# A causal mask added by VectorE on the way to its maximum, in place of matmuls

## The chip, the core and the metric

The kernel runs on one core of a Trainium2 chip. The metric is the device time of one execution in microseconds, the median of several runs.

## What is computed

16 batch entries of 128 tokens and 256 features go through four stages; x is kept in float32 and each stage adds to it.

```python
x = x + xattn0(layernorm(x), ctx, ctx)          # stage A: 32 heads of 8, 8 KV heads
x = x + moe(layernorm(x), ...)                  # stage B: top 2 of 8 experts, and a shared one
x = x + xattn1(layernorm(x), ctx, Wq, Wkv, Wo)  # stage C: 16 heads of 16, causal
x = x + ffn(layernorm(x), w1, w2)               # stage D: quantised, 256 -> 1024 -> 256
```

Stage C, which the change touches:

```python
qh, kh, vh = heads(q @ Wq.T), heads(k), heads(v)
scores = einsum('bhqd,bhkd->bhqk', qh, kh) * inv_sqrt_d
scores = where(tril(ones), scores, finfo.min)
out = einsum('bhqk,bhkd->bhqd', softmax(scores), vh) @ Wout.T
```

## The kernel before

A batch entry is a tile: 128 tokens on the 128 partitions. Each stage is cut into parts (A0 to A6, B0 to B6, C0 to C10, D0 to D4), and a part into what each engine does of it. PROGRAMS (lines 84 to 211) holds, for each engine, a hand-written list of parts with their tiles, as "C4.0/3": half 0 of part C4 of tile 3. An engine walks its list in order, and no engine looks ahead in it. So several tiles are under way at once, in different stages, and what joins the engines are semaphores. `s.wait` waits for the result of a part.

TensorE writes into two rings of PSUM slots: four small ones (one bank each) and two big ones (two banks, 1024 float32 columns). PARTS (lines 67 to 80) says for each part which ring it uses and which semaphore count frees its slot. `fill` (line 405) takes the next slot of the ring in the order of TensorE's list and waits until the part that had it before is read. The users of the big ring are A2, A4, B2, B3, B4, C4, C6 and D2.

The softmax needs each row's maximum before the exponential. Stage C finds it so:

1. C4 on TensorE (line 712), two halves of eight heads: the scores q k with the queries on the partitions, in float32 parts of bfloat16 (96 rows). Ahead of them two matmuls of 512 columns put the mask (0 or -3e38, bfloat16) into the slot through an identity, and the heads accumulate upon it.
2. C4 on VectorE (line 1220, `neg_max` at 1212): one reduce over 128x1024, straight from PSUM, gives the negated maxima of eight heads and frees the slot.
3. C4 on POOL (line 1102): the 16 maxima are split into two bfloat16 parts.
4. C5 on TensorE (line 729) transposes them, C5 on ScalarE (line 874) copies them out, C5 on the DMA queue (line 540) writes them as two more rows behind QC.
5. C6 on TensorE (line 734) makes the scores again, now with the keys on the partitions and the maximum subtracted by the two extra rows. ScalarE (line 934) takes the exponential, POOL (line 1126) sets what the mask forbids to 0, and C7 to C10 multiply by the values, normalise, project and add.

Stage A does the same in its parts A2 to A4 without a mask; its reduces (line 1214) share the helper with stage C's. Stage D's quantiser takes maxima of 256 and 1024 columns (line 1204), its D2 writes z (line 1299) and D4 scales the output (line 1308). Stage B's routing is ten small VectorE steps (lines 1244 to 1262), with two products behind them (1234, 1266), and B3 and B4 multiply by halves of 512 columns (1234, 1273).

zbuf is 2 x 1024 float32 columns. It first holds weights of stage D (f1, f2) until their signs and scales are taken, then its first half is z.

## Time and profile before

| | us |
|---|---|
| median of 3 runs | 603.13 |
| lowest, highest | 598.46, 604.03 |
| the profiled execution's own time | 601.62 |
| its span, first to last instruction | 599.6 |

The span is that of the profiled execution; 2.0 us lie around it. Durations are from this one execution. The profile gives an engine's busy time (an instruction's latency counts in it, so matmuls one behind the other overlap), the idle time in front of a group and what ended it, and the chain that ended last.

### The profile page before, as it was taken

How to read it: one execution, taken by the hardware profiler on the slowest of the kernel's cores; microseconds unless marked ns; L12 is line 12 of the kernel's file. 1: busy time of each engine (PE TensorE's matmuls, PEld its weight loads, DVE VectorE, ACT ScalarE, POOL GpSimd, SP SyncE). 2: the span in 40 equal slices, each digit the busy share in tenths (PEclk: the TensorE clock that was granted, in tenths of full speed). 3: DMA queues.
4: the chain of work that ended last, by engine and by line, in shares of the span. 5: the costliest groups of instructions: out<-in, count | busy, mean ns of one | idle time of the engine just before them, and what ended most of it. 6: DMA issues, size and time to landing. Idle time of an engine off the chain costs nothing.

```text
span 599.6 us, 10827 instructions
## 1 busy us (share of the span) xinstructions
PE 523.7 (87%) x3860; PEld 326.9 (55%) x3874; DVE 353.5 (59%) x768; ACT 397.7 (66%) x755; POOL 279.5 (47%) x536
## 2 busy tenths in 40 slices
PE   3477889899988988999799999999999999997764
PEld 1243465565655557575447565665646565674532
DVE  3643746565767674666556667576677366636342
ACT  5164344548874968575976876769677678747655
POOL 3996724365444353554435444562523443363220
PEclk9677979999999999999899999999999999999886
DMA  6788610413132220313040410432130302023000
GB/s 174 178 262 188 152 52 17 110 33 98 41 78 63 70 67 28 100 40 96 25 116 14 118 26 25 108 80 59 29 84 20 84 16 67 11 61 103 25 0 17
DMA packets 66444, 43.97 MB, mean 73 GB/s; under 512 B 36616, under 2 KB 61064, under 8 KB 66392
## 3 DMA queue, kind: packets, MB, share of 16 engines
q1 hardware_dynamic: 60064, 37.56, 24.9%
q10 hardware_dynamic: 6328, 5.73, 3.4%
q8 instruction: 31, 0.51, 0.4%
q14 instruction: 21, 0.17, 0.1%
HBM read 30.49 MB, written 12.39 MB: 71 GB/s over the span
## 4 chain that ended last, share of the span: by engine, by line
PE 54%; ACT 21%; DVE 12%; POOL 4%; issue 4%; DMA 3%; SPq 1%; POOLq 0%; ACTq 0%
PE big L651 16%; PE small L684 8%; PE small L630 4%; ACT PA L880 3%; ACT PC L880 3%; PE small L767 3%; DVE neg_maxA L1214 2%; PE big L603 2%; ACT L880 2%; PE small L588 2%; PE small L797 2%; PE big L780 2%; PE big L618 2%; PE small L749 2%; ACT g L965 2%
## 5 line engine op out<-in xcount | busy, mean ns | idle before, releaser
L1214 DVE TENSOR_REDUCE neg_maxA<-big 128x8 f32<-128x1024 f32 x64 | 77.0, 1215 | 25.6 <-PE big L603 25.1
L904 ACT ACTIVATE tB<-big,route_half 128x128 f32<-128x128 f32 x128 | 36.5, 367 | 58.9 <-PE big L651 58.9
L880 ACT ACTIVATE PA<-big 128x1024 f32<-128x1024 f32 x64 | 64.2, 1030 | 16.1 <-PE big L618 16.0
L1121 POOL TENSOR_TENSOR vB<-vB,route_c 128x512 f32<-128x512 f32 x32 | 33.3, 1039 | 82.0 <-DVE vB L1273 81.9
L684 PE MATMUL small<-w2T,hTB 128*128 128x256 f32 x288 | 66.9, 387 | 2.6 <-ACT hTB L917 2.6
L651 PE MATMUL big<-w1T,xTB 128*128 128x512 f32 x128 | 61.3, 601 | 5.2 <-DVE vB L1266 3.4
L684 PEld LDWEIGHTS small<-w2T,hTB 128*128 128x128 f32 x288 | 54.4, 193 | 11.8 <-issue 3.0
L651 PE MATMUL big<-w3T,xTB 128*128 128x512 f32 x128 | 60.2, 592 | 0.0
L1234 DVE SCALAR_TENSOR_TENSOR tB<-tB,big 128x512 f32<-128x512 f32 (+1 forms) x48 | 26.3, 548 | 41.9 <-ACT tB L904 41.9
L1129 POOL TENSOR_SCALAR_AFFINE_SELECT PC<-PC 128x1024 f32<-128x1024 f32 x32 | 35.0, 1097 | 32.4 <-ACT PC L880 32.4
L1214 DVE TENSOR_REDUCE neg_maxC<-big 128x8 f32<-128x1024 f32 x32 | 38.4, 1216 | 13.9 <-PE big L725 13.7
L651 PEld LDWEIGHTS big<-w3T,xTB 128*128 128x128 f32 x128 | 24.3, 190 | 30.6 <-issue 30.6
L651 PEld LDWEIGHTS big<-w1T,xTB 128*128 128x128 f32 x128 | 22.3, 190 | 28.0 <-issue 19.7
L603 PE MATMUL big<-KA,QA 48*128 48x128 bf16 x512 | 25.9, 229 | 12.8 <-DVE neg_maxA L1214 4.0
L880 ACT ACTIVATE PC<-big 128x1024 f32<-128x1024 f32 x32 | 32.7, 1029 | 5.0 <-PE big L740 4.8
L630 PE MATMUL small<-PA,VA 128*32 128x512 f32 x256 | 35.2, 644 | 0.7 <-ACT PA L880 0.7
L618 PE MATMUL big<-QA,KA 50*128 50x512 bf16 x128 | 25.3, 412 | 9.7 <-DVE neg_maxC L1214 3.1
L603 PEld LDWEIGHTS big<-KA,QA 48*128 48x128 bf16 x512 | 15.7, 98 | 28.9 <-DVE neg_maxA L1214 8.5
L1299 DVE SCALAR_TENSOR_TENSOR z<-big,qscale,f_scale 128x1024 f32<-128x1024 f32 x16 | 20.5, 1280 | 10.4 <-PE big L780 10.3
L888 ACT ACTIVATE OA<-small 128x512 f32<-128x512 f32 x32 | 19.3, 602 | 10.1 <-PE small L630 9.8
L917 ACT ACTIVATE hTB<-small 128x512 f32<-128x512 f32 (+1 forms) x48 | 23.4, 505 | 3.1 <-PE small L675 2.7
L675 PE MATMUL small<-ident,vB 128*128 128x128 f32 x144 | 23.3, 281 | 1.4 <-DVE vB L1266 0.8
(195 smaller groups left out, 1202.8 us busy)
## 6 DMA issues: line engine op xcount, KB each, us to landing
parts_qA<-QP SPq DMA_DIRECT2D x16, 192.0 KB, 2.4
QA<-parts_qA SPq DMA_DIRECT2D x32, 96.0 KB
parts_kC<-KPC SPq DMA_DIRECT2D x16, 192.0 KB, 2.2
KC<-parts_kC SPq DMA_DIRECT2D x16, 192.0 KB, 2.9
parts_qC<-QPC SPq DMA_DIRECT2D x16, 192.0 KB, 2.1
QC<-parts_qC SPq DMA_DIRECT2D x16, 192.0 KB, 2.9
x<-in_x SPq DMA_DIRECT2D x16, 128.0 KB, 2.4
QA<-parts_qA SPq DMA_DIRECT2D x32, 64.0 KB
```

The costliest lines, as they stand in the source:

```text
L603: last = mm(ps[:, c * BANK + g * P:c * BANK + (g + 1) * P], QA[u][rows, G0 * j + g, :], KA[rows, t // KCHUNK, j, t % KCHUNK * P:(t % KCHUN ...
L618: last = mm(ps[:, c * BANK:(c + 1) * BANK], KA[rows, t // KCHUNK, j, t % KCHUNK * P:(t % KCHUNK + 1) * P], QA[u][rows, G0 * j:G0 * (j + 1) ...
L630: last = mm(ps[SLOT * j:SLOT * (j + 1), :], VA[u][:, kv, :], PA[:, kv * G0:(kv + 1) * G0, :], start=True, stop=True)
L651: last = mm(ps[:, o:o + n], xTB[u][:, c, :], w[c], start=(c == 0), stop=(c == DC - 1))
L684: last = mm(ps[:, 0:D], hTB[:, e, :], w_2[:, e, :], start=(e == 0), stop=(e == NE - 1))
L880: return op(dst[:, 8 * j:8 * (j + 1), :], ps[:].rearrange("p (h t) -> p h t", t=P), ACT.Exp, scale=scale).then_inc(S[name], 1)
L904: ins = op(tB[:, (e0 + i) * HID:(e0 + i + 1) * HID], ps[:, i * HID:(i + 1) * HID], ACT.Tanh, scale=rt["half"][:, e0 + i:e0 + i + 1])
L917: op(hTB[:, e0:e0 + n, :], ps[:, 0:n * P].rearrange("p (e t) -> p e t", t=P), ACT.Copy)\
L1121: g.tensor_tensor(hB[:, sl].rearrange("p (e h) -> p e h", e=4), vB[:, sl].rearrange("p (e h) -> p e h", e=4), rt["c"][:, e0:e0 + 4].unsque ...
L1129: g.affine_select(out=p, in_=p, compare_op=ALU.is_ge, fill=0.0, base=0, pattern=[[0, 8], [1, P]], channel_multiplier=-1).then_inc(S["PC_ca ...
L1214: v.tensor_reduce(dst[:, 8 * j:8 * (j + 1)], ps[:].rearrange("p (h t) -> p h t", t=P), FREE, ALU.max, negate=True).then_inc(S[name], 1)
L1234: return v.scalar_tensor_tensor(out=uB[:, lo:lo + n], in0=tB[:, lo:lo + n], scalar=1.0, in1=ps[:, 0:n], op0=ALU.add, op1=ALU.mult)
```

## The change

C4 on TensorE issues no mask matmuls; each head's matmul starts and stops its own accumulation. C4 on VectorE adds the mask from SBUF to the slot and writes the sum to the second half of zbuf, named sC. It then takes the maximum from there. The slot is free after the add: PARTS names the semaphore sC for C4. The lists of parts stay. VectorE waits for its own reduce before it overwrites sC, and for its own add before it reads it; in tile 0 it also waits for the mask and for zbuf. TensorE's wait for the constants goes from C4 to C6.

```diff
-    ... "C4.0": (1, "nmC", 2, 1),
-    "C4.1": (1, "nmC", 2, 2), ...
+    ... "C4.0": (1, "sC", 2, 1),
+    "C4.1": (1, "sC", 2, 2), ...
-        z = zbuf[:, 0, :]
+        z, sC = zbuf[:, 0, :], zbuf[:, 1, :]
...
             def C4(s, t, u, j):
                 ps, full = s.fill()
-                if t == 0 and j == 0:
-                    pe.wait_ge(S["consts"], 3)
                 if j == 0:
                     s.landed("KC_in", t, 3)
                     s.landed("QC_in", t, 3)
-                for b in range(2):
-                    mm(ps[:, b * BANK:(b + 1) * BANK], identb[:], mask[:].unsqueeze(1).broadcast_to([P, 4, P]),
-                       start=True, stop=False)
-                for b in range(2):
-                    for i in range(4):
-                        h = 8 * j + 4 * b + i
-                        last = mm(ps[:, b * BANK + i * P:b * BANK + (i + 1) * P], QC[u][0:K1, h, :], KC[u][0:K1, h, :],
-                                  start=False, stop=(i == 3))
+                for i in range(8):
+                    h = 8 * j + i
+                    last = mm(ps[:, i * P:(i + 1) * P], QC[u][0:K1, h, :], KC[u][0:K1, h, :], start=True, stop=True)
                 last.then_inc(full, 1)
...
             def C6(s, t, u, j):
                 ps, full = s.fill()
+                if t == 0 and j == 0:
+                    pe.wait_ge(S["consts"], 3)
...
             def C4(s, t, u, j):
-                neg_max(s, j, nmC[u], "nmC")
+                ps = s.read()
+                if t == 0 and j == 0:
+                    dve.wait_ge(S["consts"], 3)
+                    dve.wait_ge(S["f2_sign"], 2)
+                if t or j:
+                    dve.wait_ge(S["nmC"], 2 * t + j)
+                heads = sC.rearrange("p (h t) -> p h t", t=P)
+                v.tensor_tensor(heads, ps[:].rearrange("p (h t) -> p h t", t=P), mask[:].unsqueeze(1).broadcast_to([P, 8, P]),
+                                ALU.add).then_inc(S["sC"], 1)
+                dve.wait_ge(S["sC"], 2 * t + j + 1)
+                v.tensor_reduce(nmC[u][:, 8 * j:8 * (j + 1)], heads, FREE, ALU.max, negate=True).then_inc(S["nmC"], 1)
```

## Rows read from the trace of the kernel before

**Rows 1.** The page's first part: busy time, share of the span, instructions.

```profile
PE 523.7 (87%) x3860; PEld 326.9 (55%) x3874; DVE 353.5 (59%) x768; ACT 397.7 (66%) x755; POOL 279.5 (47%) x536
```

**Rows 2.** Stretches: us; engines' busy us; TensorE's granted clock, DMA share, GB/s.

```profile
130.00:545.00 415.00, 387.83 (x2998) 250.01 (x3009) 260.74 (x587) 302.97 (x587) 191.04 (x375) 1.00 0.24 60
200.00:300.00 100.00, 91.93 (x714) 58.10 (x716) 64.19 (x139) 73.02 (x140) 45.62 (x95) 0.98 0.25 63
545.00:575.00 30.00, 23.16 (x221) 14.28 (x220) 14.54 (x26) 20.04 (x26) 10.28 (x19) 0.94 0.19 50
575.00:600.00 25.00, 13.04 (x62) 6.99 (x63) 9.12 (x20) 13.77 (x18) 2.45 (x5) 0.73 0.03 10
```

**Rows 3.** The page's chain that ended last, by engine.

```profile
PE 54%; ACT 21%; DVE 12%; POOL 4%; issue 4%; DMA 3%; SPq 1%; POOLq 0%; ACTq 0%
```

**Rows 4.** Groups by line, TensorE: busy us, mean ns | idle before.

```profile
L720 PE MATMUL big<-mask,identb 128*128 128x512 bf16 x64 | 19.2, 381 | 1.2 <-ACT PA L880 0.5 <-DVE z L1299 0.5 <-ACT PC L880 0.2
...
L732 PE MATMUL small<-identb,neg_max2C 128*32 128x128 bf16 x16 | 3.6, 226 | 0.1
```

**Rows 5.** Timeline, tile 0's C4: start us, duration, instruction.

```profile
109.30 0.59 PE L720 MATMUL big<-mask,identb 128*128 128x512 bf16 x2
109.73 0.61 PE L725 MATMUL big<-KC,QC 96*128 96x128 bf16 x8
...
110.38 2.35 DVE L1214 TENSOR_REDUCE neg_maxC<-big 128x8 f32<-128x1024 f32 x2 [2.52 <-PE big L725]
...
112.98 0.63 PE L651 MATMUL big<-sw1T_gateT,xTB 128*128 128x136 f32 x4
```

**Rows 6.** Groups by line, VectorE.

```profile
L1214 DVE TENSOR_REDUCE neg_maxC<-big 128x8 f32<-128x1024 f32 x32 | 38.4, 1216 | 13.9 <-PE big L725 13.7
...
L1273 DVE TENSOR_TENSOR vB<-tB,big 128x512 f32<-128x512 f32 x32 | 22.0, 687 | 1.1
L1299 DVE SCALAR_TENSOR_TENSOR z<-big,qscale,f_scale 128x1024 f32<-128x1024 f32 x16 | 20.5, 1280 | 10.4 <-PE big L780 10.3
L1204 DVE TENSOR_REDUCE qscale<-g 128x1 f32<-128x1024 f32 x16 | 19.4, 1210 | 6.3 <-ACT g L965 6.3
...
L1290 DVE TENSOR_TENSOR oC<-small,rlC 128x256 f32<-128x256 f32 x16 | 6.8, 424 | 0.6
```

**Rows 7.** Line 1179: duration ns min/median/max, first and last start.

```profile
L1179 DVE SCALAR_TENSOR_TENSOR f2q<-g,f2q x1: 1601/1601/1601, 46.5 to 46.5; 128x1024 bf16<-128x1024 f32 x1
```

**Rows 8.** Timeline, C4, C5, C6 of tiles 14 and 15.

```profile
549.30 1.21 DVE L1214 TENSOR_REDUCE neg_maxC<-big 128x8 f32<-128x1024 f32 x1
...
550.42 1.21 DVE L1204 TENSOR_REDUCE qscale<-g 128x1 f32<-128x1024 f32 x1
...
551.21 0.22 PE L732 MATMUL small<-identb,neg_max2C 128*32 128x128 bf16 x1
...
551.66 0.15 DVE L1205 TENSOR_SCALAR qscale<-qscale 128x1 f32<-128x1 f32 x1
...
556.76 0.62 PE L740 MATMUL big<-QC,KC 98*128 98x128 bf16 x8 [0.76 <-DMA QC<-neg_maxT_C]
...
558.30 1.23 DVE L1214 TENSOR_REDUCE neg_maxC<-big 128x8 f32<-128x1024 f32 x1 [1.05 <-PE big L725]
...
561.99 0.22 PE L732 MATMUL small<-identb,neg_max2C 128*32 128x128 bf16 x1
...
563.14 1.86 PE L797 MATMUL small<-f2q,gT 128*128 128x256 bf16 x8 [0.93 <-ACT gT L976]
```

**Rows 9.** Timeline, C4 and C5 of tile 2.

```profile
169.05 2.35 DVE L1214 TENSOR_REDUCE neg_maxC<-big 128x8 f32<-128x1024 f32 x2 [2.69 <-PE big L725]
...
172.42 0.23 PE L732 MATMUL small<-identb,neg_max2C 128*32 128x128 bf16 x1
```

**Rows 10.** Timeline, TensorE behind C5 of tile 6.

```profile
293.52 0.23 PE L732 MATMUL small<-identb,neg_max2C 128*32 128x128 bf16 x1
...
295.24 0.40 PE L603 MATMUL big<-KA,QA 48*128 48x128 bf16 x8 [1.48 <-ACT PA L880]
```

More of the change, by code:

```diff
@@ L377, in build @@
             "xTC", "qTC", "kTC", "VC", "qpC", "kpC", "qpC_out0", "qpC_out1", "kpC_out0", "kpC_out1", "QC_in0", "QC_in1", "KC_in0", "KC_in1",
-            "nmC", "nm2C", "mTC", "mrowsC", "PC", "PC_causal", "OC", "rlC", "oC", "oTC", "x3_done",
[1 row of a table added]
             "qs1", "yq", "yT", "z", "g", "g2", "gq", "gT", "y2", "x4_done")}
```

5 rows, old and new, of tables (PARTS, S) are left out of this document.

## The prediction, made before the change was run

> **What bounds the kernel now.** I read the page's busy line first [rows 1]: TensorE is busy 87% of the span, VectorE 59%, ScalarE 66%. The table of stretches then says where [rows 2]: between 130 and 545 us TensorE is busy 387.8 of 415 us, 93%, at a granted clock of 1.00, ScalarE 73% and VectorE 63%. From 545 us on TensorE is busy 77%, then 52%. The chain of work that ended last is 54% TensorE, 21% ScalarE, 12% VectorE [rows 3]. So TensorE, walking a fixed list of parts, sets the pace in the middle; behind 545 us it is the latency of one tile's chain, and VectorE lies in it.
>
> That seems to invite the change, for it takes work from TensorE and gives it to an engine with 246 us of idle time. But TensorE's list is in order, and it waits for VectorE's result four parts or so after it asked for it. So the question is how much room there is between the end of C4's maxima and the part C5 that transposes them.
>
> **What goes.** Each of the 32 C4 parts loses two mask matmuls of 512 columns. The group shows 381 ns for one, 19.2 us busy in all [rows 4], but that counts the latency of each part's first matmul; what they hold is the distance between starts: 109.30 for the masks, 109.73 for the heads behind them, 0.43 us [rows 5]. That is 32 x 0.43 = 13.8 us of TensorE. They stand behind all of C4's waits, so no wait hides them. The eight head matmuls stay as they are.
>
> **What comes.** Each C4 gains one VectorE add, 128x1024 in float32, PSUM and the bfloat16 mask in, SBUF out. No such row exists. The nearest are adds and products with one operand in PSUM: 687 ns for 512 columns, 424 for 256 [rows 6], so 1.03 ns a column and 1.21 us for 1024. The one-operand pass over 1024 from PSUM takes 1.22, the three-operand one 1.28. The low end is 0.69 us, the 512-column row, if repeating the short mask over the heads somehow halved the price; the high end is 1.60 us, the slowest pass over 1024 with bfloat16 in it [rows 7]. I take 1.21, the row of the same kind. The reduce now reads SBUF: the same length from SBUF takes 1.21 against 1.22 [rows 6], no change.
>
> The two self-waits: behind a reduce the next instruction without a wait starts 1.12 us after it (549.30, 550.42), the one that waits for it 1.24 (550.42, 551.66) [rows 8]. So add to reduce is 1.24, and a pair that stands together goes from 2.35 to 3 x 1.24 + 1.21 = 4.93 us: 2.6 more. VectorE in all gains 32 x 1.27 = 41 us, 353 to 394, 65% of the span; no bound by itself. The page "VectorE: DVE Perf Modes" of the Trainium skill, section "The DRAIN you can't avoid", says that a semaphore between two operations costs nothing extra. By it the pair would be 4 x 1.12 + 0.09 = 4.57, a third of a microsecond less a tile. The two starts above speak against it, so the sum keeps 1.24.
>
> The waits on the mask's constants and on the staging buffer fall on tile 0 at 110 us, when both are long done; the last pass that needs the signs is over by 49 us [rows 7]. The mask wait moved to C6 costs nothing for the same reason. POOL's select behind the exponentials stays, and no DMA is added.
>
> **What it does to the order.** The PSUM slot now comes free after the add (1.21) and no more after the reduce (1.22). For the first C4 of a pair that is no loss and, where VectorE waited for TensorE, 0.43 early. For the second it comes one reduce later. The result of the pair is late by D: 2.6 where the pair stands together and VectorE was busy anyway; 2.6 - 0.43 = 2.15 where it waited for the matmuls, as in tile 2 [rows 9]; 1.24 or 0.8 where only the second reduce still matters, because the two stand apart.
>
> The shortest way from a reduce's end to C5 is 0.70 us (550.51 to 551.21 [rows 8]): two POOL instructions and their semaphores. Slack is C5's start less the reduce's end less 0.70. Tile 2 is the type [rows 9]: reduces end at 171.40, C5 at 172.42, slack 0.32, D = 2.15, so C5 starts 1.8 later than before, and TensorE, which would have been there 0.86 early, stands for 2.7. Behind it in VectorE's list come C10, D0, D4 and two reduces of stage A; they are 2.15 late as well, which is no worse than C5.
>
> By the same reading of all 16 tiles (C4's and C5's rows, of which [rows 5, 8, 9, 10] show the first, the last two, a typical one and an absorbed one), TensorE is later than before by: tile 0 0.7 (C5 has 4 us of slack, but B2 wants the slot of the second C4 at 112.98 and gets it at 110.38 - 0.43 + 2 x 1.24 + 1.21 = 113.64 [rows 5]); 1 0.7; 2 1.8; 3 0.8; 4 0.4; 5 0.1; 6 0.65; 7 0.6; 8 0.2; 9 0; 10 1.3; 11 0.5; 12 -0.5 (slack 4.1, the gain stays); 13 1.3. Tile 6 shows why it isn't D less slack everywhere, which would be 2.3 there: TensorE stood for 1.48 us before 295.24, until ScalarE had read a PSUM slot [rows 10], so 1.7 of the 2.3 vanish. The sum is 8.6 us. The 13.8 us of TensorE are already in it: each C5 comes 0.86 early, and that time is spent waiting.
>
> Tiles 14 and 15 are on the chain. For tile 14 the last chain runs through VectorE: z, maximum, quantiser, maximum, quantiser, then ScalarE [rows 8]. Two adds and their waits go in, 2 x 1.24 = 2.5 us, nothing hides them; the other way out, C5 to the row DMA to C6 at 556.76, was waited for too and is as late. Tile 15: add from 557.87, reduce until 560.32, D4's pass of 0.48, add from 560.8, reduce until 563.3, C5 at 564.0 in place of 561.99; but D4 behind it in TensorE's list waited until 563.14 for ScalarE anyway, so 0.9 [rows 8]. Together 3.4 us.
>
> Of the 8.6 us some comes back. Between 130 and 545 us TensorE is idle 27 us [rows 2], many of the pieces waits for ScalarE, which doesn't slow down. A TensorE that is 1 us late finds such a wait 1 us shorter, as at tile 6. I let half return: 4.3 + 3.4 = 7.7 us. The span goes to 607.3, and with the 2.0 us around it (601.62 against 599.6) to 609.3. The profiled execution lay 1.5 us under the median of the runs shown (603.13); from that median the forecast is 610.8. I give 610, +1.1%.
>
> **Rivals.** (a) TensorE's gain wins, faster. It needs the waits at C5 to be short: an add well under 1.2 us, or the pieces of slack growing because all other parts of VectorE get ahead. Then 13.8 us times TensorE's busy share in the middle, 0.93, less the 3.4 us of the tail, -9.5: about 592 to 595. For it speaks that TensorE is the busiest engine and VectorE has a third of its time free; against it the slack under 1 us in ten of 16 tiles. It decides where the second result is late by less than about 0.8 us. Chance 0.13.
> (b) All cancels in the middle: ScalarE's waits take up the whole 8.6, and only the tail is left: +3, 605 to 606. Chance 0.27. ScalarE's 73% in the middle speaks for it [rows 2].
> (c) VectorE's lateness spreads, slower by much more. Each second C4 holds up what is behind it in the list: stage A's 64 reduces, which free the two large PSUM slots, and the ten small routing steps before B2's products, which are on the chain today. If tiles that stand together pay the full 2.6 and those apart 1.2 with nothing coming back, 7 x 2.15 + 9 x 0.8 less what is hidden gives +15 to +20: 617 to 622. A little of it could be TensorE's clock: the whole middle has 1.00 at 93% busy, the stretch from 200 to 300 us 0.98 at 92% [rows 2], and 2% of a slower clock on a stretch of 100 us is at most 2 us. Against (c): VectorE is idle over 3 us in every 10. Chance 0.15.
> (d) That the change doesn't take the matmuls away, or that they cost nothing today, I exclude: they have rows of their own, and nothing waits in front of them for more than 1.2 us in all [rows 4].
>
> **The numbers.** Forecast 0.45, with its own range of 605 to 616. A measurement of this kernel tells about 1% from no change, that is 597.1 and 609.2. Faster is (a), 0.13. Within 1%: (b) and a third of the forecast's share, 0.25 + 0.13 = 0.38. Slower the rest, 0.49. The range for 8 in 10 takes in (b) and most of (c), and leaves out (a): 600 to 619. The ends of the add's price (0.69, 1.60) move the sum by 32 x 0.4 x about a third, some 4 to 6 us, which fits inside.
>
> **What would show it.** Right: C5's transpose (line 732, moved) has a wait for POOL's copy of the maxima of 1 to 2.5 us in most tiles, some 15 to 20 us in all, where before it had 0.1 [rows 4]; TensorE's busy time falls by 14 to 19 us and its idle time grows by more; the add takes 1.2 us, VectorE is busy some 392 us; the stretch from C4 of tile 14 to the end is 3 us longer. Wrong: no wait at C5, TensorE's busy share unchanged in the middle and the span shorter (then a), or C5's waits there, but ScalarE's waits of TensorE gone and the span the same (then b).

## The result, and the profile after

The changed kernel takes 620.97 us (median of 4 runs, 619.31 to 622.37), the kernel before 602.0 on the same chip (598.46 to 604.03): a ratio of 1.0322, 95% interval 1.0276 to 1.0368. So 19 us slower, where the forecast was 610 us (7.7 us more of span) with a range of 600 to 619. A ratio is taken over the single runs of a kernel and of the kernel before on the same chip, and can lie up to 0.3% beside that of the medians. A few executions fall into a slower state of the chip and stay out of every ratio, here two of x8's ten, its profiled one among them. The profiled execution took 620.25 us, its span is 618.5, 18.9 more than before. First the page's busy line and its chain by engine:

```profile
PE 518.8 (84%) x3796; PEld 323.3 (52%) x3810; DVE 390.7 (63%) x800; ACT 398.9 (64%) x755; POOL 279.4 (45%) x536
...
PE 47%; DVE 24%; ACT 16%; issue 5%; DMA 4%; POOL 3%; SPq 1%; POOLq 0%; DVEq 0%
```

VectorE's busy time is up by 37.2 us (the adds are 39.0), and its share of the chain has doubled against [rows 3]. TensorE's busy time fell by 4.9 us only [rows 1]. Span less busy time is its idle time: 75.9 us before, 99.7 now. These 23.8 us less 4.9 are the 18.9 of the span, so the place to look is what ends TensorE's waits. Groups by line (line, operation, out<-in, count | busy us, mean ns | idle time before them, and what ended it):

```profile
L725 PE MATMUL small<-identb,neg_max2C 128*32 128x128 bf16 x16 | 3.7, 229 | 11.4 <-POOL neg_max2C L1089 11.4
...
L618 PE MATMUL big<-QA,KA 50*128 50x512 bf16 x128 | 25.7, 419 | 15.3 <-DVE z L1224 8.0 <-DMA QA<-neg_maxT_A 3.3 <-ACT PA L875 2.6
...
L588 PE MATMUL small<-ident,oC 128*128 128x128 f32 x32 | 6.6, 287 | 3.2 <-DVE oC L1296 3.1
...
L719 PE MATMUL big<-KC,QC 96*128 96x128 bf16 x256 | 19.4, 220 | 3.5 <-ACT PA L875 1.3 <-ACT PC L875 1.0 <-DVE z L1305 0.9
```

The first is C5, where the forecast looked: 11.4 us of waiting in place of 0.1 [rows 4]. The second is a part of stage A (A4, its second scores matmul) that fills a large PSUM slot. In the kernel before the same group reads:

```profile
L618 PE MATMUL big<-QA,KA 50*128 50x512 bf16 x128 | 25.3, 412 | 9.7 <-DVE neg_maxC L1214 3.1 <-ACT PA L880 2.6 <-DMA QA<-neg_maxT_A 2.3
```

So it waits 5.6 us more, and what grew is the wait until C4 has read its slot, from 3.1 to 8.0 us. The third stands behind VectorE's normalisation of stage C (0.4 before). The fourth is C4 itself (1.2 before, on the mask's row [rows 4]). So half of the new idle time, 11.3 of 23.8 us, stands at C5, the other half elsewhere.

VectorE's two new groups, and the timeline of tile 2, which the prediction took as its type [rows 9]:

```profile
L1224 DVE TENSOR_TENSOR z<-big,mask 128x1024 f32<-128x1024 f32 x32 | 39.0, 1218 | 7.8 <-PE big L719 6.9
...
L1227 DVE TENSOR_REDUCE neg_maxC<-z 128x8 f32<-128x1024 f32 x32 | 39.0, 1220 | 1.1
```

```profile
170.47 0.62 PE L719 MATMUL big<-KC,QC 96*128 96x128 bf16 x8 [0.52 <-ACT PA L875]
171.13 1.22 DVE L1224 TENSOR_TENSOR z<-big,mask 128x1024 f32<-128x1024 f32 x1 [2.25 <-PE big L719]
171.38 0.62 PE L719 MATMUL big<-KC,QC 96*128 96x128 bf16 x8 [0.29 <-ACT PA L875]
172.23 0.41 PE L588 MATMUL small<-ident,xnC 128*128 128x128 f32 x2 [0.23 <-ACT xnC L856]
172.39 1.22 DVE L1227 TENSOR_REDUCE neg_maxC<-z 128x8 f32<-128x1024 f32 x1
...
173.71 1.23 DVE L1224 TENSOR_TENSOR z<-big,mask 128x1024 f32<-128x1024 f32 x1
...
174.97 1.22 DVE L1227 TENSOR_REDUCE neg_maxC<-z 128x8 f32<-128x1024 f32 x1
...
176.91 0.21 PE L725 MATMUL small<-identb,neg_max2C 128*32 128x128 bf16 x1 [1.91 <-POOL neg_max2C L1089]
```

The starts of add, reduce, add, reduce are 1.26, 1.32 and 1.26 us apart, and the pair takes 5.06 us (171.13 to 176.19) for 2.35 before. TensorE, ahead by the four mask matmuls that are gone (0.86 us), spends 0.29 and 0.23 us of that on two new waits for ScalarE, and then waits 1.91 us at C5.

The middle, as in [rows 2]:

```profile
130.00:545.00 415.00, 370.60 (x2846) 237.66 (x2857) 287.31 (x600) 295.09 (x567) 181.79 (x360) 0.99 0.23 57
```

In the middle TensorE is busy 89% in place of 93%. The end, tiles 14 and 15, from the timeline:

```profile
565.90 1.23 DVE L1224 TENSOR_TENSOR z<-big,mask 128x1024 f32<-128x1024 f32 x1
...
567.16 1.22 DVE L1227 TENSOR_REDUCE neg_maxC<-z 128x8 f32<-128x1024 f32 x1
...
569.08 0.27 PE L725 MATMUL small<-identb,neg_max2C 128*32 128x128 bf16 x1 [1.58 <-POOL neg_max2C L1089]
...
577.92 1.21 DVE L1224 TENSOR_TENSOR z<-big,mask 128x1024 f32<-128x1024 f32 x1
...
579.17 1.22 DVE L1227 TENSOR_REDUCE neg_maxC<-z 128x8 f32<-128x1024 f32 x1
...
581.09 0.26 PE L725 MATMUL small<-identb,neg_max2C 128*32 128x128 bf16 x1 [0.80 <-POOL neg_max2C L1089]
```

C5 of tile 15 is 19.1 us later than in [rows 8]. The table below gives that for every second tile or so: the start of C5's matmul in this kernel's timeline less its start before. It has four of the experiments too, which come later.

```
tile                                0    2    4    6    8   10   12   13   15
changed kernel                    1.7  4.5  6.9  9.4  9.6 11.3 13.7 15.4 19.1
x1  no mask, no add               0.7  2.3  3.1  2.4  2.1  1.2  0.8  0.8  0.7
x14 no mask in tiles 7-13         2.5  2.5  2.5  2.4  2.8  1.9  1.6  1.5  1.5
x9  spare reduce behind C4's      1.6  2.3  5.3  7.5  9.7 10.1 12.4 12.5 14.7
x12 spare reduce ahead of C4's    5.1  7.7  9.1 12.9 16.2 18.5 21.5 22.6 25.9
```

Read the steps along a row, not its first number (each is one execution): x14 runs the same instructions as before up to tile 6 and is 2.5 us late from the start, which is the difference between two executions.

One step of the changed kernel is not VectorE's. From tile 3 to tile 4 it loses 1.9 us, and 1.6 of them lie in one group of 18 matmuls of stage B (line 684), which took 4.12 us before. First the kernel before, then the changed one, with a stretch inside the group. Third from its end stands the granted clock, the share of TensorE's full speed of 2.4 GHz that it was given:

```profile
225.96 4.12 PE L684 MATMUL small<-w2T,hTB 128*128 128x256 f32 x18 [0.55 <-ACT hTB L917]
```

```profile
231.00 5.75 PE L684 MATMUL small<-w2T,hTB 128*128 128x256 f32 x18 [0.93 <-ACT hTB L912]
...
232.00:236.00 4.00, 4.00 (x15) 3.35 (x14) 0.32 (x3) 3.96 (x6) 1.10 (x1) 0.71 0.00 0
```

The clock fell there. In windows of 4 us between 100 and 545 us the trace of before has one such fall (296 to 300 us), the changed kernel's has four (108, 228, 300 and 448 us, each some 8 us long). TensorE's busy time in each such window, times what is missing of the full clock, is 1.6 us in all before and 6.0 now.

### The profile page after: what moved, and what is told of

The parts are those of the page before. It is cut to its first block, busy times and chain, and to the rows that moved or that the text cites. A ratio compares the mean times of both kernels' runs of the same rounds, so it can differ in the third digit from the quotient of the medians.

```text
span 618.5 us, 10763 instructions
## 1 busy us (share of the span) xinstructions
PE 518.8 (84%) x3796; PEld 323.3 (52%) x3810; DVE 390.7 (63%) x800; ACT 398.9 (64%) x755; POOL 279.4 (45%) x536
## 4 chain that ended last, share of the span: by engine, by line
PE 47%; DVE 24%; ACT 16%; issue 5%; DMA 4%; POOL 3%; SPq 1%; POOLq 0%; DVEq 0%
PE big L651 15%; PE small L684 8%; DVE z L1224 5%; DVE neg_maxC L1227 5%; PE small L630 4%; DVE neg_maxA L1209 3%; ACT PA L875 2%; PE small L762 2%; ACT PC L875 2%; PE big L603 2%; PE big L775 2%; ACT g L960 2%; PE big L618 1%; PE small L705 1%; PE small L675 1%
## 5 line engine op out<-in xcount | busy, mean ns | idle before, releaser
L1224 DVE TENSOR_TENSOR z<-big,mask 128x1024 f32<-128x1024 f32 x32 | 39.0, 1218 | 7.8 <-PE big L719 6.9
L1227 DVE TENSOR_REDUCE neg_maxC<-z 128x8 f32<-128x1024 f32 x32 | 39.0, 1220 | 1.1
L883 ACT ACTIVATE OA<-small 128x512 f32<-128x512 f32 x32 | 19.1, 601 | 9.7 <-PE small L630 9.7
```

The lines of the kernel that those rows point to most:

```text
L1224: v.tensor_tensor(heads, ps[:].rearrange("p (h t) -> p h t", t=P), mask[:].unsqueeze(1).broadcast_to([P, 8, P]), ALU.add).then_inc(S["sC"], 1)
L1227: v.tensor_reduce(nmC[u][:, 8 * j:8 * (j + 1)], heads, FREE, ALU.max, negate=True).then_inc(S["nmC"], 1)
```

## The experiments

Three things were open. Which part of the 19 us is VectorE's load, which is C4's result being late, and which its PSUM slots? What is the taking of 13.8 us from TensorE worth? And what has TensorE's clock to do with it, since its mean is 0.938 to 0.946 in the runs of the changed kernel and 0.955 in the profile of before?

### The two halves of the change, each alone

**x1: the masks' matmuls gone, no add.** The kernel before, its C4 without the mask matmuls. The maxima are then over all keys; the select behind the exponentials still masks.

```diff
-                for b in range(2):
-                    mm(ps[:, b * BANK:(b + 1) * BANK], identb[:], mask[:]...)
...
+                for i in range(8):
+                    h = 8 * j + i
+                    last = mm(ps[:, i * P:(i + 1) * P], QC[u][0:K1, h, :], KC[u][0:K1, h, :], start=True, stop=True)
```

> The kernel before without its mask matmuls, and with no add: the maximum is taken over all keys, also those that the causal mask forbids (the select behind the exponentials still sets those to 0). It measures what TensorE's part of the change is worth alone. If TensorE's 13.8 us count in full where it sets the pace: 589 to 591 us against 602. If TensorE only comes earlier to waits for others, so that the saving is worth little: 598 to 602. The changed kernel's 621 is then this time plus what VectorE's add costs.

Measured: 603.57 us (10 runs) beside 601.38, ratio 1.001 (0.9975 to 1.0045). 13.8 us less of TensorE's work changed nothing clear of the noise (1.5 us less to 2.7 more), which is near the second of the two expectations. Groups of this run:

```profile
L618 PE MATMUL big<-QA,KA 50*128 50x512 bf16 x128 | 24.9, 402 | 12.4 <-DVE neg_maxC L1209 5.1 <-DMA QA<-neg_maxT_A 3.1 <-ACT PA L875 2.6
...
L721 PE MATMUL big<-KC,QC 96*128 96x128 bf16 x256 | 19.4, 219 | 3.7 <-ACT PA L875 1.3 <-ACT PC L875 1.1 <-DVE z L1294 0.9
...
L727 PE MATMUL small<-identb,neg_max2C 128*32 128x128 bf16 x16 | 3.6, 227 | 0.5 <-POOL neg_max2C L1089 0.5
```

C5 hardly waits, so its slack was there. But the slots' waits grew from 9.7 to 12.4 us and C4's own from 1.2 to 3.7: TensorE gets to a slot sooner and finds it not yet read.

**x2: both.** The changed kernel with the mask matmuls put back as before (the lines that x1 takes out); the mask's constant is -1e38 in place of -3e38, since it is now added twice.

> The changed kernel with the mask matmuls put back in front of the heads (the mask is added twice, at -1e38 each, so no value overflows): VectorE's part of the change alone. If the two parts simply add up, this is 621 plus what the matmuls' removal is worth: 632 to 634 if that is 12 us, 623 if it is 2. If the removal made the waits at C5 longer (TensorE comes 0.86 us a tile too early and stands there), its worth in this company is far less than alone: 621 to 625 while the kernel without any mask is at 590.

Measured: 629.39 us (4 runs), ratio 1.0441 (1.039 to 1.0492), so VectorE's half of the change costs 26 to 28 us by itself. From x2 to the changed kernel (1.0441 to 1.0322) the same matmuls are worth some 7 us, give or take 4, and alone nothing. The two halves don't add, and x2 lies between the two cases that were expected.

**x4 and x5: one C4 of the two.** The add for the first (x4) or the second C4 of each tile only (x5), the other one as before.

```diff
             def C4(s, t, u, j):
+                if j != 0:          # x5: j != 1
+                    return neg_max(s, j, nmC[u], "nmC")
                 ps = s.read()
```

> The change for the first half of C4 alone: its mask is added by VectorE, the second half keeps its mask matmuls, its plain reduce and its slot freed by the reduce. The theory of the joints (what counts is how late C5's input and the second slot are) expects little where the two halves stand apart, for the first add is then over long before: 603 to 608. The theory of the load (each microsecond on VectorE costs its share wherever it lies) expects half of the whole change: 610 to 612.

> The change for the second half of C4 alone. Its add lies between the matmuls and C5 in every tile. The theory of the joints expects most of the loss here: 612 to 617. The theory of the load expects the same as for the first half, 610 to 612.

Measured: x4 609.71 us, ratio 1.012 (1.0096 to 1.0145); x5 610.69 us, ratio 1.0129 (1.0088 to 1.0171), 4 runs each. By the medians that is 8.3 and 9.3 us, together 17.6 of the 19; by the ratios 7.2 and 7.8, together 15.0 of 19.4. An add in front of the first maximum costs about as much as one in front of the second. Had the lateness of the tile's result been all, the first would have to be the cheaper one, since where the two C4 stand apart only the second reduce matters to C5: 603 to 608 us were expected for it by that, against 612 to 617. The intervals (1.5 us either way for x4, 2.5 for x5) leave room for a small difference only.

### VectorE's load against its late result

**x9 and x12: a spare reduce.** The kernel before, with one more VectorE reduce for each C4, over 8x127 columns of an idle staging buffer, that nobody reads. In x9 it stands behind C4's reduce, so C4's first slot and maxima are in time (the second only where the two stand apart) and what is behind comes 1.2 us later; in x12 ahead of it, behind the wait for the matmuls, so that every slot and maximum of C4 is later by 1.2 us more. The masks stay on TensorE.

```diff
             def C4(s, t, u, j):
                 neg_max(s, j, nmC[u], "nmC")
+                ...
+                v.tensor_reduce(zbuf[:, 1, HF - 8:], zbuf[:, 1, 0:HF - 8].rearrange("p (h t) -> p h t", t=P - 1), FREE, ALU.max,
+                                negate=True).then_inc(S["sC"], 1)      # x12: ahead of neg_max, behind s.read()
```

> The kernel before, mask matmuls and all, with a spare VectorE reduce over 8x127 columns of the idle staging buffer behind each C4 reduce (its result is used by nobody): 32 x 1.2 us more on VectorE, but C4's own slot and maxima come as before, except where the second half stands directly behind the first one's spare. If it is VectorE's load that costs, whatever the microseconds are spent on: 625 to 630, as VectorE's part of the change alone (629). If it is the lateness of C4's own results: 605 to 612.

> The same spare reduce ahead of each C4 reduce, behind the wait for the matmuls: the same load, and C4's slot and maxima 1.2 us a half later. Load theory: the same time as with the spare behind. Theory of late results: 635 to 642, since here the slot is late as well (that cost 11 us in the changed kernel).

Measured: x9 614.01 us, ratio 1.0195 (1.0145 to 1.0245); x12 624.95 us, ratio 1.0374 (1.0319 to 1.043); 4 runs each, beside 601.96. So 38.4 us of load behind the results cost 12.0 us, and in front of them another 10.9. Neither theory had this: 614 lies between what late results (605 to 612) and load (625 to 630) gave for x9, 625 between what they gave for x12. Nor is x9 load alone, since in the eight tiles where the two C4 stand together its second slot and maxima are 1.2 us late. First x9's groups, then x12's:

```profile
L1226 DVE TENSOR_REDUCE z<-z 128x8 f32<-128x1016 f32 x32 | 38.4, 1201 | 0.0
...
L618 PE MATMUL big<-QA,KA 50*128 50x512 bf16 x128 | 26.0, 424 | 12.5 <-DVE neg_maxC L1214 5.4 <-DMA QA<-neg_maxT_A 3.4 <-ACT PA L880 2.4
...
L732 PE MATMUL small<-identb,neg_max2C 128*32 128x128 bf16 x16 | 3.7, 232 | 1.2 <-POOL neg_max2C L1094 1.1
```

```profile
L618 PE MATMUL big<-QA,KA 50*128 50x512 bf16 x128 | 25.3, 412 | 21.5 <-DVE neg_maxC L1214 13.0 <-DMA QA<-neg_maxT_A 4.5 <-ACT PA L880 2.4
...
L732 PE MATMUL small<-identb,neg_max2C 128*32 128x128 bf16 x16 | 3.7, 230 | 7.4 <-POOL neg_max2C L1094 7.3
```

In x9 C5 waits 1.2 us in all, and the kernel is still 12 us slower; the slot group waits 2.8 us more than before, the rest is spread over other groups. In x12 the slot group alone waits 9 us more than in x9, C5 6.2 more.

**x3: the slot.** The changed kernel, but the PSUM slot counts as free only when the reduce is done, not the add.

```diff
-... "C4.0": (1, "sC", 2, 1), "C4.1": (1, "sC", 2, 2), ...
+... "C4.0": (1, "nmC", 2, 1), "C4.1": (1, "nmC", 2, 2), ...
```

> The changed kernel with C4's PSUM slot freed by the reduce and not by the add: the same work and order, the slot 1.24 us later. It prices the slots. If the big ring is a joint that counts: 630 to 640, for 32 slots are each 1.24 us later. If VectorE's load alone counts: 621 to 624.

Measured: 631.73 us (4 runs), ratio 1.05 (1.0443 to 1.0557), against 1.0322: slots that come some 1.26 us later cost 11 us more, as the theory of the slots had it (630 to 640).

```profile
L618 PE MATMUL big<-QA,KA 50*128 50x512 bf16 x128 | 24.8, 401 | 22.1 <-DVE neg_maxC L1227 16.7 <-ACT PA L875 2.4 <-DVE neg_maxA L1209 1.5
...
L725 PE MATMUL small<-identb,neg_max2C 128*32 128x128 bf16 x16 | 3.9, 244 | 7.6 <-POOL neg_max2C L1089 7.5
```

The slots' wait for C4 doubles from 8.0 to 16.7 us; C5's shrinks from 11.4 to 7.6, for TensorE is already late when it gets there.

**x6: C5 later in TensorE's list.** The changed kernel with C5 one to four parts later in 14 tiles (for tile 2: behind A2.3, A5.0 and A5.1 in place of ahead of them).

```diff
-        C4.0/2 C4.1/2 C1/3 C10/1 B1/4 D4/0 A2.2/6 C5/2 A2.3/6 A5.0/5 A5.1/5 A2.0/7 ...
+        C4.0/2 C4.1/2 C1/3 C10/1 B1/4 D4/0 A2.2/6 A2.3/6 A5.0/5 A5.1/5 C5/2 A2.0/7 ...
```

> The changed kernel with C5 moved one to six parts later in TensorE's list in 14 of the 16 tiles (not 1 and 14), so that up to about 2 us of other matmuls come ahead of it. It takes away the waits of C5 for the maxima (11.4 us in the changed kernel). If C5's waits are what the change costs: 609 to 612 against 621. If the cost is VectorE's load, met at whatever joint comes next: 618 to 622, with C5's waits gone and others longer.

Measured: 629.64 us (4 runs), ratio 1.0473 (1.0409 to 1.0536), 9 us worse than the change it was to mend, and outside both expectations (609 to 612, 618 to 622). In this kernel line 726 is C5:

```profile
L726 PE MATMUL small<-identb,neg_max2C 128*32 128x128 bf16 x16 | 3.8, 238 | 3.6 <-POOL neg_max2C L1090 3.6
...
L652 PE MATMUL big<-w1T,xTB 128*128 128x512 f32 x128 | 63.5, 620 | 7.4 <-DVE vB L1273 5.5 <-DVE neg_maxA L1210 1.9
...
L652 PE MATMUL big<-sw1T_gateT,xTB 128*128 128x136 f32 x64 | 12.4, 321 | 3.6 <-ACT PA L876 1.6 <-DVE neg_maxA L1210 1.0 <-ACT xTB L888 1.0
```

C5's wait went from 11.4 to 3.6 us, and other parts, wait longer (line 652: 7.4 and 3.6 for 5.1 and 1.3). Moved in this way, the wait at C5 was where the lateness showed, not where it could be taken off; other orders were not tried.

**x11: both adds first.** The changed kernel with the masked scores in bfloat16, so that two fit the staging buffer; in the eight tiles where the two C4 stand together the order is add, add, reduce, reduce, and no instruction waits for the one right ahead of it.

```diff
+                if together and j == 0:
+                    return
+                for i in ((0, 1) if together else (j,)):
+                    dve.wait_ge(S["sC"], 2 * t + i + 1)
+                    v.tensor_reduce(nmC[u][:, 8 * i:8 * (i + 1)], heads[i], FREE, ALU.max, negate=True).then_inc(S["nmC"], 1)
```

> The changed kernel with sC in bfloat16, two of them in the same bytes, so that in the seven tiles whose halves stand together (0, 1, 2, 5, 6, 7, 10, 13: eight with 5) VectorE does both adds first and then both reduces: the second slot comes free 1.24 us earlier, the first maximum 1.24 later, the last as before. In the other tiles nothing moves. Slots as a joint that counts (11 us for 32 slots 1.24 us later): 3 us less, 617 to 618. Load: 621.

Measured: 619.55 us (4 runs), ratio 1.029 (1.0242 to 1.0338); the interval overlaps the change's. Tile 2 in its timeline:

```profile
169.24 2.36 DVE L1226 TENSOR_TENSOR z<-big,mask 128x1024 bf16<-128x1024 f32 x2 [2.26 <-PE big L719]
171.51 2.33 DVE L1232 TENSOR_REDUCE neg_maxC<-z 128x8 f32<-128x1024 bf16 x2
```

The four take 4.60 us (169.24 to 173.84) in place of 5.06. Eight tiles of 0.46 us are 3.7 us of latency less, of which 1.4 show, and these are within the error: x11 can't tell the 617 to 618 of the slots from the 621 of the load.

### Shortening in place of lengthening

**x8 and x10.** x8 is the kernel before with C4's reduce over 64 of each head's 128 keys, which takes 16 us off VectorE (337.7 us busy in x10's profile, 353.5 before; a piece of the computation is left out); x10 is x8 and x1 together.

```diff
-                neg_max(s, j, nmC[u], "nmC")
+                ps = s.read()
+                v.tensor_reduce(nmC[u][:, 8 * j:8 * (j + 1)], ps[:].rearrange("p (h t) -> p h t", t=P)[:, :, 0:P // 2], FREE, ALU.max,
+                                negate=True).then_inc(S["nmC"], 1)
```

> The kernel before with C4's reduce cut to the first 64 of 128 keys of each head (the maximum leaves out the other keys; nothing else changes): VectorE has 32 x 0.53 = 17 us less to do. VectorE's part of the change cost 28 us for 40 us of work, 0.7 for 1. If that slope holds in both directions, VectorE paces the kernel already: 602 - 12 = 590. If the order of the lists is fitted to today's durations, so that longer hurts and shorter doesn't help, as with the mask matmuls: 599 to 602.

> The kernel before with both cuts at once: no mask matmuls (the maximum takes in forbidden keys) and C4's reduce over 64 of 128 keys. TensorE has 13.8 us less, VectorE 17 us less. Each alone gave nothing. If the two engines' lists hold each other, so that each alone only waits longer for the other: 588 to 595. If something else holds both (ScalarE, whose list is untouched, or the chain of one tile at the end): 599 to 603.

Measured: x8 601.12 us beside 602.78, ratio 0.9974 (0.9935 to 1.0012); x10 602.1 us beside 601.96, ratio 1.0001 (0.9971 to 1.0032), 10 runs each. Neither engine's work, nor both together, gives anything clear of the noise when it shrinks, as the expectation of fitted lists had it.

### The clock

**x7: C5's waits filled.** The changed kernel with 42 dummy matmuls ahead of C5 and C9 in the tiles where they wait, so that TensorE is busy there.

```diff
-    A4.0/1:10 C2.1/0:4 ...
+    C5/1:2 C5/2:7 C5/3:2 C5/6:3 C9/4:4 C5/10:6 C9/8:3 C9/11:2 C5/13:5 C5/14:6 C5/15:2 A4.0/1:10 C2.1/0:4 ...
```

> The changed kernel with 42 idle matmuls (the kernel's own fillers, 512 columns, result unused) put into the waits of C5 and C9 that its trace shows, each a little shorter than the wait. It adds no work that matters and keeps TensorE active. If part of the loss is TensorE's granted clock (0.94 over the runs of the changed kernel, 0.96 over those of before): the clock rises to 0.95 or more and the time falls to 613 to 617. If the clock plays no part: 621, or 1 to 3 us more.

Measured: 622.33 us (4 runs), ratio 1.0362 (1.0299 to 1.0426). The granted clock of the four runs is 0.946 to 0.958, against 0.938 to 0.946, and the time is not better. The clock rose as foretold for the case that it is part of the loss, but the 613 to 617 us of that case did not come; 622 is what was expected if the clock plays no part. The C5 group:

```profile
L725 PE MATMUL small<-identb,neg_max2C 128*32 128x128 bf16 x16 | 3.7, 234 | 3.6 <-POOL neg_max2C L1089 2.9 <-ACT gT L971 0.7
```

**x13 and x14: where the masks go.** With all masks gone (x1) the clock fell to about half (0.50 to 0.53 in windows of 2 us) in three places of the middle, before only in one (296 to 300 us). x13 leaves the masks out in 13 tiles and keeps them in tiles 2, 4 and 6, just ahead of those places; x14 leaves them out in tiles 7 to 13 alone, where x1's clock stood at 1.00. Maxima over all keys in the tiles without masks.

```diff
-                for b in range(2):
-                    mm(...mask...)
+                if t in (2, 4, 6):          # x14: t < 7 or t > 13
+                    ...as before
+                else:
+                    ...as x1
```

> The kernel before with the mask matmuls left out in 13 tiles (26 x 0.43 = 11.2 us of TensorE less) and kept in tiles 2, 4 and 6, just ahead of the three stretches in which TensorE's granted clock fell when all were gone (168 to 176, 228 to 232, 296 to 304 us: together about 6.8 us of TensorE at full clock, against 1.7 before). In those 13 tiles the maxima are over all keys; the select behind the exponentials still masks. If the clock ate the gain, the falls at 168 and 228 are away, the transpose of the maxima is no more 1.6 and 1.4 us late behind tiles 2 and 4, and the time is 3 to 5 us under that with all masks gone: 598 to 600. If waits side by side ate it, moving a fall changes little: the same time as with all gone, 601 to 604, the lateness per tile about as before at +1 to +3.

> The kernel before with the mask matmuls left out in tiles 7 to 13 only (14 x 0.43 = 6.0 us of TensorE less, maxima over all keys there), where the clock stood at 1.00 with all of them gone. The parts ahead of tile 7 run as before, with the one fall at 296. If the clock is what takes the gain elsewhere, most of the 6 us shows by tile 13's transpose of the maxima: 3 to 5 us early, 597 to 599. If waits for ScalarE and VectorE take it, as in the run with all gone (from 2.8 late at tile 7 to 0.8 at tile 13, 2.0 us gained by six tiles), 2 us early or less, and 600 to 602 in all.

Measured: x13 601.39 us, ratio 0.9993 (0.9975 to 1.001); x14 599.73 us, ratio 0.9965 (0.9946 to 0.9984), beside 601.76, 12 runs each. x14 is the only kernel of the study whose interval lies below the one before, by 2.0 us (1.0 to 3.3). First x1's stretches (granted clock third from the end), then x13's, x14's, and the last of the kernel before:

```profile
172.00:176.00 4.00, 4.00 (x37) 2.38 (x40) 2.56 (x5) 1.19 (x3) 1.93 (x5) 0.77 0.10 33
228.00:232.00 4.00, 4.00 (x12) 3.23 (x11) 0.17 (x2) 3.99 (x5) 0.66 (x1) 0.57 0.00 0
...
344.00:520.00 176.00, 166.60 (x1303) 106.67 (x1302) 114.87 (x257) 133.97 (x253) 78.32 (x151) 1.00 0.21 54
```

```profile
172.00:176.00 4.00, 4.00 (x47) 2.60 (x49) 3.93 (x8) 2.19 (x6) 1.59 (x6) 1.00 0.44 99
228.00:232.00 4.00, 4.00 (x26) 3.35 (x26) 0.36 (x2) 3.99 (x5) 0.79 (x1) 1.00 0.00 0
```

```profile
344.00:520.00 176.00, 165.96 (x1292) 106.61 (x1295) 115.47 (x262) 133.90 (x252) 77.67 (x149) 1.00 0.21 54
```

```profile
344.00:520.00 176.00, 167.89 (x1321) 108.32 (x1326) 113.15 (x250) 133.80 (x252) 77.93 (x150) 1.00 0.20 53
```

In x13 the falls at 172 and 228 us are away, and tiles 2 and 4 don't step back by 1.6 and 1.4 us as in x1. But other falls came, at 112 and 336 us, and in all they take as much as x1's: TensorE's busy time times the missing clock, in the windows of 4 us, is 6.1 us in x13, 5.9 in x1, 2.6 in x14. So x13 moved the falls and did not lessen them, and its time is the one expected if moving a fall changes little (601 to 604), not the 598 to 600 of the other case.

The stretch from 344 to 520 us shows what the waits alone do: the clock is 1.00 in all three kernels, and TensorE is idle 8.1 us before, 9.4 in x1, 10.0 in x14.

Between C5 of tile 7 and C5 of tile 13 six tiles lose 6 x 0.86 = 5.2 us of matmuls. This way takes 182.4 us in the kernel before, 180.4 in x1 and x13, 180.8 in x14; x13 and x14 have the end of a fall of the clock in it, 0.4 and 0.7 us of busy time at what is missing. So 2.0 to 2.3 of the 5.2 us reach the end at a full clock, about 40%. Over the same way TensorE's idle time goes from 8.3 us to 9.6 to 10.0, and its busy time falls by 3.2 to 4.1 only, the clock's part put aside. So new waits take 1.3 to 1.7 us, and the last 1 to 2 us never leave the busy time. Part of a wait may be counted there, since an instruction's latency counts as busy; that is not shown. x14's result fits the case that was expected if waits take the gain (2 us early or less by tile 13) and not the one in which the clock takes it.

**All runs by their clock.** Each run has its mean granted clock beside its time. Taken as deviations from the mean of their own kernel (154 runs, the befores of each chip as a kernel of their own), time goes with the clock by -348 us for 1.0 (standard error 27, correlation -0.74): a clock lower by 0.01 goes with 3.5 us more. By that slope each kernel's difference from before splits into a part with the clock and a rest:

```
kernel                        us over before   median clock (before)   with clock   rest
x1   13.8 us of PE less             +0.6         0.944  (0.958)          +4.9       -4.3
x13  11.2 us of PE less             -0.4         0.9495 (0.958)          +3.0       -3.4
x14   6.0 us of PE less             -2.1         0.958  (0.958)           0.0       -2.1
x8   16 us of DVE less              -1.6         0.960  (0.955)          -1.7       +0.1
x10  x1 and x8                      +0.1         0.946  (0.961)          +5.2       -5.1
x4   add for the first C4           +7.2         0.950  (0.958)          +2.8       +4.4
x5   add for the second C4          +7.8         0.9535 (0.958)          +1.6       +6.2
x9   38.4 us of DVE behind         +11.7         0.956  (0.961)          +1.7      +10.0
x12  38.5 us of DVE ahead          +22.5         0.956  (0.961)          +1.7      +20.8
x2   adds, masks kept              +26.5         0.9375 (0.958)          +7.1      +19.4
changed kernel                     +19.4         0.9405 (0.958)          +6.1      +13.3
x11  adds first                    +17.5         0.9405 (0.961)          +7.1      +10.4
x7   waits filled                  +21.8         0.947  (0.955)          +2.8      +19.0
x6   C5 later                      +28.5         0.938  (0.955)          +5.9      +22.6
x3   slots late                    +30.1         0.9365 (0.955)          +6.4      +23.7
```

(Microseconds over before are the ratio less one, times 602; for the changed kernel the clock of before is the middle of the others. The intervals of the ratios alone are 1 to 4 us either way, so a rest is good to some 2 us at best.) The three kernels with masks left out come to one third: 4.3 of 13.8, 3.4 of 11.2, 2.1 of 6.0, each within 2 us of error, and near what the way at full clock shows. Read so, x1 has two answers in it: two thirds of what TensorE saved never reached the end, and the clock took what was left. Its trace agrees in size, with falls that count 4.4 us more than before's. That a lower clock lengthens a run is shown where a fall covers one group (4.12 to 5.75 us). That all of the slope is this cause, and not in part longer waits that lower the clock, is not shown. x7 speaks against it: dummy matmuls raised the clock by 0.0065, the time didn't fall, and its rest is 19.0 us for the changed kernel's 13.3. But it can't decide, since they are themselves work on the path, and x13 and x14 did not come out as the clock alone would have it.

## Why the prediction was wrong in its size

**Right.** The direction, and that VectorE's part decides the matter and TensorE's saving does not (x2 and x1). The add: 1.218 us for 1.21, the reduce from SBUF 1.220 for 1.21, VectorE busy 390.7 us for 392 to 394. The pair took 5.06 us for 4.93, for the instruction that waits for the one ahead of it started 1.26 to 1.32 us after it and not 1.24. The tail: tile 13's C5 is 15.4 us late, tile 14's 17.9, which is the 2.5 of the forecast, and the span ends 18.9 late, 3.5 us after tile 13's lateness for a forecast of 3.4. By the rule of the Trainium skill ("VectorE: DVE Perf Modes", "The DRAIN you can't avoid") that the prediction weighed, the pair would have been at 4.57. The changed kernel's 5.06 speaks against it where a result is waited for; x11's 4.60, with the waits one instruction further back, is what the rule gives.

**The sum in the middle.** Forecast against measured, the lateness that each tile adds at its C5, from the same two timelines as the table:

```
tile        0    1    2    3    4    5    6    7    8    9   10   11   12   13   sum
forecast  0.7  0.7  1.8  0.8  0.4  0.1 0.65  0.6  0.2  0.0  1.3  0.5 -0.5  1.3   8.6
measured  1.7  0.9  1.9  0.5  1.9  0.3  2.2 -0.5  0.7  0.7  1.0  1.4  1.0  1.6  15.4
```

Tiles 1, 2, 3, 5 and 10 are within 0.3 us of the forecast, 6 and 7 together within 0.4. The falls of the clock lie in tiles 0 (108 us), 4 (228), 6 and 7 (300) and 11 (448), and of the four misses of 0.9 us or more that are left three are in these tiles, 0, 4 and 11 (tile 0's 1.7 also has the difference between two executions in it). The fourth is tile 12, whose gain of 0.5 us didn't stay.

**"I let half return: 4.3."** The first step that failed. One return was real, and the forecast had it, at tile 6 [rows 10]. There before, TensorE stood for 1.48 us behind C5 and again for 0.74:

```profile
296.38 1.27 PE L780 MATMUL big<-f1q,yT 128*128 128x512 bf16 x3 [0.74 <-ACT PA L880]
```

In the changed kernel it is

```profile
298.39 0.39 PE L618 MATMUL big<-QA,KA 50*128 50x512 bf16 x2 [0.91 <-DVE z L1224]
...
300.98 0.39 PE L618 MATMUL big<-QA,KA 50*128 50x512 bf16 x2 [2.19 <-DVE z L1224]
...
302.88 0.27 PE L725 MATMUL small<-identb,neg_max2C 128*32 128x128 bf16 x1 [0.96 <-POOL neg_max2C L1089]
303.07 0.61 PE L603 MATMUL big<-KA,QA 48*128 48x128 bf16 x8
304.02 1.48 PE L775 MATMUL big<-f1q,yT 128*128 128x512 bf16 x3 [0.34 <-issue]
```

and from C5 to that matmul (now line 775) it takes 1.14 us where it took 2.86: the 1.7 us that the prediction wrote off. To let half of the remaining 8.6 return as well was to count on more such waits without a row for one. None came: but for tile 7, where that one return shows, the changed kernel is later tile after tile, 15.4 us by tile 13, and 11.0 without the 4.4 that its falls of the clock count more. With the return struck out, the forecast's own sum is 8.6 + 3.4 = 12.0 us, and by the slope the rest at the same clock is 13.3, the same within the error.

**"2% of a slower clock on a stretch of 100 us is at most 2 us."** The second step that failed. The clock was looked at for one stretch, inside a rival, and had no term in the sum. The changed kernel's runs have 0.0175 less of it, which goes with 6.1 us by the slope of all runs, and the falls of its trace count 4.4 us more than before's. If that is the clock's doing, which is argued and not shown, these two steps, 4.3 and 4.4 to 6.1, are most of the distance between the forecast's 7.7 and the 19 measured.

**"No worse than C5."** Of the parts behind C4 the prediction said that they are late as well, but no worse than C5. The lines above show one that is worse: the second scores matmul waits 0.91 and 2.19 us for the slot of C4's add, and over the kernel that wait grew from 3.1 to 8.0 us (the forecast read the slot in tile 0 only, at B2). x3 prices that joint, 11 us for slots 1.26 us later, and x9 the load behind: 10 to 12 us with hardly a wait at C5. In the changed kernel the sum came out within 1.3 us of the C5 reading all the same. That is partly luck: C5 waited for less than forecast and the slots for more. What rival (c) named (lateness that spreads through stage A's slots) did happen, and its 617 to 622 us held the result, though by the slope a third of the 19.4 us goes with the clock, which the rival had at 2 us at most.

**"The 13.8 us of TensorE are already in it."** That most of them would be lost in waits came true: x2 to the changed kernel is 26.5 to 19.4, 7 us of 13.8. Rival (a), with 0.93 of them gained, is ruled out by x1: alone they gave nothing (0.6 us over before), and at the same clock, by the slope, a third.

**The signs foretold.** C5's waits: 11.4 us in all, 0.3 to 1.9 in twelve tiles, for 15 to 20. TensorE's busy time was to fall by 14 to 19 us and fell by 4.9 (x1 4.0, x10 8.0). Of the missing 9 us the falls of the clock, which stretch the busy time, are 4.4. The rest is of the kind seen at a full clock, where 5.2 us of masks took only 3.2 to 4.1 us off the busy time between tiles 7 and 13.

**Slips of count.** Rival (c) has the two C4 together in seven tiles; in VectorE's list it is eight (0, 1, 2, 5, 6, 7, 10 and 13). And 32 x 1.27 us for VectorE's gain takes its waits in; 32 adds of 1.21 are 38.7, and 39.0 were measured.

**What stays open.** Whether the slope between time and clock is all the clock's doing. And why the clock falls where it does: x13 moved the falls without lessening them and x14 had a new one at 336 us, but no run here shows what sets the place.

## What to carry to other kernels

Where engines walk lists that were fitted to each other, less work on the busiest one reaches the end in part only (here a third to 40%) and more on another costs 0.3 us per microsecond if it lies behind the results and 0.6 if ahead of them: read the slack at each joint, the PSUM slots too, and let nothing return without a row for it. Give TensorE's clock a term of its own in the sum whenever an edit takes matmuls away or adds waits, and set every run's mean clock beside its time before saying what an edit is worth; x1 looked like nothing gained and, if the slope is the clock's, held a gain of 4.3 us and a loss of 4.9. The only edit that gained left work out where the clock stood at full and nowhere else (x14, 2 us faster than the kernel before). It isn't the same computation: its maxima also take in the keys that the mask forbids, which is safe only as long as no forbidden score lies so far above the others that their exponentials vanish.

## What was not expected of the hardware

Taking 13.8 us of matmuls out of 524 lowered the mean granted clock of TensorE from 0.952 to 0.963 (13 runs of before) to 0.941 to 0.950 (10 runs of x1); taking 6.0 us out of tiles 7 to 13 left it at 0.952 to 0.961 (before on that chip: 0.955 to 0.966, the median of both is 0.958). The spread of one kernel's times, 598 to 605 us for before, goes with that clock by a correlation of -0.70 over 62 runs, which is half of the variance.

The add writes bfloat16 in the same time as float32, and the reduce reads it no faster: in x11 two adds take 2.36 us and two reduces 2.33, where one of each over float32 takes 1.22 (means over the kernel: 1.215 and 1.215 for 1.218 and 1.220).
